# Order of the query tiles in a causal attention stage: each head from its longest row block to its shortest

## The reference

```python
q = (x @ Wq.T).reshape(B, T, H, hd)
...
q = _rmsnorm(q, gq)
k = _rmsnorm(k, gk)
...
scores = jnp.einsum('bhqd,bhkd->bhqk', q, k) * scale
...
scores = jnp.where(mask[None, None], -jnp.inf, scores)
attn = jax.nn.softmax(scores.astype(jnp.float32), axis=-1).astype(q.dtype)
out = jnp.einsum('bhqk,bhkd->bhqd', attn, v)
out = out.transpose(0, 2, 1, 3).reshape(B, T, H * hd)
return out @ Wo.T
```

## Time and profile before

| what | value |
|---|---|
| median of 3 runs | 1378.33 us (1376.38 to 1378.66) |
| the profiled execution, its own time | 1382.27 us |
| its span, first to last instruction | 1380.5 us |
| mean granted TensorE clock | 0.942 of full speed |
| PE busy | 1231.5 us, 89% of the span |
| PEld busy | 946.4 us, 69% |
| DVE busy | 962.3 us, 70% |
| ACT busy | 707.0 us, 51% |
| POOL busy | 552.5 us, 40% |
| chain that ended last | PE 54%, DVE 29%, issue 9%, ACT 5% |

### The profile page before, as it was taken

How to read it: one execution, slowest core, us unless ns; L and a number is a source line. 1 busy time by engine, 2 the same in 40 slices (tenths; PEclk the granted TensorE clock), 3 DMA queues, 4 the chain that set the end, 5 groups by cost and what they waited for, 6 DMA issues and landing times.

```text
span 1380.5 us, 24347 instructions
## 1 busy us (share of the span) xinstructions
PE 1231.5 (89%) x7708; PEld 946.4 (69%) x7708; DVE 962.3 (70%) x2821; ACT 707.0 (51%) x1639; POOL 552.5 (40%) x509
## 2 busy tenths in 40 slices
PE   6889888886469999999989999999998999999998
PEld 5435454443447787777877877778786788777787
DVE  5766777765467868778778678686677676675553
ACT  3354645455336456465464565554564654645442
POOL 0200000000038988898889888887802200000000
PEclk9799898888579999999999999999999999999999
DMA  6411011001110002101102001012001100000000
GB/s 216 123 30 46 24 43 55 24 32 62 61 55 23 32 11 101 41 0 41 41 10 91 21 27 39 8 38 96 4 30 62 34 32 23 8 0 1 16 16 31
DMA packets 31893, 56.85 MB, mean 41 GB/s; under 512 B 7096, under 2 KB 23328, under 8 KB 31312
## 3 DMA queue, kind: packets, MB, share of 16 engines
q1 hardware_dynamic: 27696, 42.93, 9.3%
q0 software_dynamic: 2976, 8.90, 2.2%
q10 hardware_dynamic: 1152, 4.19, 0.8%
HBM read 44.23 MB, written 11.66 MB: 40 GB/s over the span
## 4 chain that ended last, share of the span: by engine, by line
PE 54%; DVE 29%; issue 9%; ACT 5%; DMA 1%; SPq 1%; DVEq 0%; ACTq 0%
PE bank L1364 11%; PE bank L1342 7%; PE bank L278 6%; PE bank L280 6%; PE bank L279 6%; DVE qkst L1022 5%; DVE qk L1041 4%; PE bank L1353 4%; PE bank L1332 2%; DVE negmax L968 2%; PE bank L1277 2%; PE bank L1246 2%; DVE negmax L1054 2%; ACT hN L326 2%; PE bank L1264 1%
## 5 line engine op out<-in xcount | busy, mean ns | idle before, releaser
L574 POOL TENSOR_SCALAR gtmp<-gidx,lut 128x344 f32<-128x344 int32 (+2 forms) x210 | 302.8, 1442 | 21.3
L577 POOL TENSOR_TENSOR gacc<-gacc,gtmp 128x344 f32<-128x344 f32 (+2 forms) x210 | 183.4, 874 | 17.5
L1342 PE MATMUL bank<-kT,qT 128*128 128x128 f32 (+3 forms) x512 | 179.8, 442 | 9.4 <-ACT probs L776 9.4
L1364 PE MATMUL bank<-pT,v 128*128 128x128 f32 x1280 | 155.5, 277 | 12.3 <-ACT pT L769 12.3
L776 ACT ACTIVATE probs<-bank,negmax 128x128 f32<-128x128 f32 (+3 forms) x256 | 135.6, 530 | 53.6 <-DVE negmax L1054 50.9
L1054 DVE TENSOR_REDUCE negmax<-bank 128x1 f32<-128x128 f32 (+3 forms) x256 | 123.6, 485 | 54.9 <-PE bank L1343 53.5
L1364 PEld LDWEIGHTS bank<-pT,v 128*128 128x128 f32 x1280 | 148.0, 192 | 16.2 <-DVE oL L1064 14.9
L968 DVE TENSOR_REDUCE negmax<-bank 128x1 f32<-128x512 f32 (+3 forms) x176 | 108.9, 636 | 67.5 <-PE bank L1266 66.6
L1022 DVE BATCH_NORM_STATS2 qkst<-qk 128x6 f32<-128x128 f32 x512 | 110.2, 281 | 61.7 <-issue 61.6
L278 PE MATMUL bank<-wgH,hL 128*128 128x512 f32 x384 | 152.9, 398 | 0.2 <-issue 0.2
L280 PE MATMUL bank<-wgH,hH 128*128 128x512 f32 x384 | 153.0, 399 | 0.0
(11 more groups left out here) (215 smaller groups left out, 2707.2 us busy)
## 6 DMA issues: line engine op xcount, KB each, us to landing
hH<-h_saved SPq DMA_DIRECT2D x16, 512.0 KB, 3.8
hL<-h_saved SPq DMA_DIRECT2D x16, 512.0 KB, 4.8
qst<-q_parts SPq DMA_DIRECT2D x96, 64.0 KB, 2.3
wg<-in_wqkv SPq DMA_DIRECT2D x4, 1536.0 KB, 8.3
gate<-gates POOLq DMA_DIRECT2D x4, 512.0 KB, 7.0
wo<-in_wo SPq DMA_DIRECT2D x4, 512.0 KB, 9.1
out<-x SPq DMA_DIRECT2D x8, 256.0 KB, 2.1
wmod<-in_wmod SPq DMA_DIRECT2D x1, 1536.0 KB, 10.7
```

Of the source, the lines that this page charges most:

```text
L574: link(pool.tensor_scalar(tmp if j else acc, part, float(j), lut1[0:rows, j:j + 1], ALU.is_equal, ALU.mult))
L577: link(pool.tensor_tensor(acc, acc, tmp, ALU.add))
L1342: pe.matmul(bank[SCORE_BANKS[i % 3]][:, 0:n], qT[:, h, t * P:n], kT[:, h, 0:n], start=True, stop=False)
L1364: last = pe.matmul(bank[7][:, t * P:(t + 1) * P], v1[:, k, h * HD1:(h + 1) * HD1], pT1[:, h % 2, at:at + P], start=(k == 0), stop=(k == t))
```

## The change

A function `item1` gives the head and the tile of an item; t now goes 3, 2, 1, 0 within a head. All three engines use it: for the number of columns, for the place in `pT1`, and for the number of transposes. Slots, lags, buffers and the tests `i % QT == QT - 1` for the last item of a head stay. The wait of the first scores on `tr_act` is now one wait, at item 0, for all 8 steps.

```diff
+def item1(i):
+
+    return i // QT, QT - 1 - i % QT
...
-                        h, t = i // QT, i % QT
+                        h, t = item1(i)
                         act.wait_ge(t1_pe, it * ITEMS + i + 1)
                         act.wait_ge(pv1, it * HG + max(h - 1, 0))
                         at = t * (t + 1) // 2 * P
...
-                        n = (i % QT + 1) * P
+                        n = (item1(i)[1] + 1) * P
                         act.wait_ge(max1, it * ITEMS + i + 1)
...
-                        n = (i % QT + 1) * P
+                        n = (item1(i)[1] + 1) * P
                         dve.wait_ge(rsum1, it * ITEMS + i + 1)
...
-                        i, n = s, (s % QT + 1) * P
+                        i, n = s, (item1(s)[1] + 1) * P
                         dve.wait_ge(s1_pe, it * ITEMS + i + 1)
...
-                        i, h, t = s, s // QT, s % QT
+                        i, (h, t) = s, item1(s)
                         n = (t + 1) * P
-                        if i < QT:
-                            pe.wait_ge(tr_act, it * 2 * QT + 2 * (t + 1))
+                        if i == 0:
+                            pe.wait_ge(tr_act, (it + 1) * 2 * QT)
                         pe.wait_ge(exp1, it * ITEMS + max(i - 2, 0))
...
-                        t = i % QT
+                        t = item1(i)[1]
                         if i == 0:
                             pe.wait_ge(x1_add, it * 2)
```

## The result

The changed kernel takes **1457.01 us** (median of 6 runs, 1449.63 to 1457.99) against 1377.36 us for the kernel before (6 runs, 1375.29 to 1380.63). The ratio is 1.0558, with a 95% interval of 1.0540 to 1.0575. It is 79.6 us slower by the medians; the ratio and its interval make it 76.9 us (74.4 to 79.2), so the medians stand just above its upper edge. The forecast was 1438 us in a range of 1407 to 1460: the sign, the mechanism and the range held, and the forecast of +59.5 us was 20 us short of the difference of the medians.

The account below looks back on a forecast made before the run. TensorE bounds the kernel, never waiting within a head. Terms +32.5, +19.7, +18.9, -17.0 and +5.4 us sum to +59.5 us, taking the median of 1378.33 to 1437.8, taken as 1438 us; range 1407 to 1460.

Parts of the forecast that it names:

- the quiet terms: Costs without GpSimd over 16 rounds: starts +32.5 us, third heads +19.7 us, fourth heads with the end +18.9 us.
- the terms for GpSimd: Old starts' idle time where VectorE is late given back, -17.0 us; 512-column scalings slowed beside GpSimd, +5.4 us.
- the rival with GpSimd in the way: Every 512-column scaling in 11 rounds takes 1.08 instead of 0.49 us, 26 instead of 5.4 us: 1458 us; chance 8%.
- Cover of T3: 512-column item's transposes, within a head: due 3.06 us after its scores start instead of 5.29, as PV now follows them.
- Chain with `oH` and `oL` ahead of the scaling: 512-column softmax from the third head on: transposes start 4.29 us after the scores instead of 3.06; TensorE waits 1.23 us.
- The rival "`oH` and `oL` not on the path": Both slip beside the softmax chain, so the 512-column transposes wait 0.32 us in every head: 1409 us; chance 8%.
- End of a round, +1.18 us: Last head's 512-column scores to the last PV's end: 11.49 instead of 10.31 us, as the last PV waits for oL.
- Start, +2.03 us: Round's start: 512-column scores come first and need all copies; third head begins 2.03 us later, +32.5 us in 16 rounds.
- "Less what the old starts lose": Round starts where VectorE is late: 9.4 us before scores and most of 10.3 us behind the scaling go, -17.0 us.
- GpSimd's +5.4 us: 512-column scaling beside GpSimd takes 610 instead of 487 ns, on the path four times in each of about 11 rounds.
- The last round: a term put at nothing: Next stage's norm in the same queues, before and after: costed at nothing, bound of a microsecond or two.
- No loss of clock: TensorE waits of 1.2 us in 32 heads and 1.4 us at round ends are too short to lower the clock.

Follow-up runs that it names:

- run 8: Both kernels with 15 of the 16 GpSimd table entries left out of the feed-forward weights: kernel before 1351.58 us, changed kernel 1430.00 us.
- run 1: Changed kernel with oL one slot later on VectorE, behind the 512-column scaling instead of ahead of it: 1455.83 us.
- runs 3 and 4: Changed kernel with PV in two banks by turns and, in the first, oL one slot later (1430.36 us); in the second, oH and oL two slots later (1419.00 us).
- runs 6 and 7: Changed kernel with, in the first, only each round's first head in the old order (1427.89 us); in the second, only that head in the new order (1398.30 us).

## Why the prediction was right, and 20 us short

The mechanism was right, to some hundredths of a microsecond in a quiet head; the size of the sum was not. Its 59.5 us become the measured 79.6 by four parts: +7.4 in the quiet terms, +6.8 in the terms for GpSimd, +1.2 ahead of the rounds, and +4.7 because the profiled execution of before stood above its median. The measured 1457 is also what the rival with GpSimd in the way had (1458). That is a coincidence of numbers: by that rival GpSimd would add 26 - 17 = 9 us net to the difference, and run 8 puts it between -5 and +1.

- **Cover of T3, 3.06 us after S3 instead of 5.29: right.** T3 waits 1.05 us by the profile's count, 1.2 against the pitch of a queue without gaps, and a head takes 7.00 to 7.01 where 6.97 was forecast.
- **Chain with `oH` and `oL` ahead of the scaling: right as a reading of the path**, T3 at 4.28 against 4.29. What the prediction didn't see is that the single PV bank is a second limit of the same height: run 1 took `oL` out of the chain, the head stayed at 7.07 to 7.16 us and nothing was gained; runs 3 and 4 took both and gained 27 and 38 us. The rival "`oH` and `oL` not on the path" was priced at 1409; the nearest run, with both out of it, gave 1419.
- **End of a round, +1.18 us with the fourth head's wait inside it: right.** Third to last PV is 4.52 us, and the steps gave 9.26 - 4.74 = 4.52.
- **Start, +2.03 us: a little small.** In quiet rounds the last copy of k to the first PV takes 7.95 us; the steps gave 7.71. I had taken the pitch of a queue without gaps. The first S3 takes 1.02 us to the next start (1244.11 to 1245.13, below) instead of 0.91, and a T3 behind a wait up to 0.04 us more than its 0.45. In all, the quiet terms were 71.1 us, and the traces without lookups show 78.5: a quiet round costs 4.8 instead of 4.4 us, which is 5 of the 7 us, and the last round 6.3.

```profile
1244.11 1.13 PE L1347 MATMUL bank<-kT,qT 128*128 128x512 f32 x2 [0.83 <-ACT kT L765]
...
1245.13 0.86 PE L1347 MATMUL bank<-kT,qT 128*128 128x384 f32 x2
...
1246.88 0.49 PE L1347 MATMUL bank<-kT,qT 128*128 128x128 f32 x2 [0.29 <-ACT probs L781]
...
1247.65 0.63 PE L1358 MATMUL bank<-identf,probs 128*128 128x128 f32 x4 [0.22 <-issue]
```

- **"Less what the old starts lose", -17.0 us: the step that failed.** The size of the old loss was right: 110.1 - 92.2 = 17.9 us in the starts. Wrong was "there the new S3 comes no later than the first maximum allows", as if the new start had no such loss. It has 135.9 - 129.4 = 6.5 us of its own, so 11.4 came back and not 17.0. Ahead of the starts (first column) the new order loses another 1.4 us more than the old.
- **GpSimd's +5.4 us: the size held.** Between the PV the new order loses 2.9 and 3.6 us to GpSimd, the old one 0.7, 0.1 and 0.5, net 5.2; the forecast had the first two heads in it as well, whose part lies in the 6.5 us above. But the way was not an even one. In some rounds the scaling that T3 waits for falls beside GpSimd's work head after head, and lasts 1.12 us each time:

```profile
552.67 1.12 DVE L1054 TENSOR_SCALAR probs<-probs,rsum 128x512 f32<-128x512 f32 x1
...
560.33 1.12 DVE L1054 TENSOR_SCALAR probs<-probs,rsum 128x512 f32<-128x512 f32 x1
```

  These two are one head apart, and T3 waits 1.70 us in both. Both later heads were hit in rounds 3, 4 and 6 of the sixteen and one of them in some others, not all four scalings in all eleven rounds as the rival for GpSimd assumed. The net of the two GpSimd terms was forecast at -11.6 us; it is -4.8 by the rounds of the four traces and +1.2 by the medians of the four kernels.
- **The last round: a term put at nothing.** The prediction gave the norm of the next stage a bound of a microsecond or two. That round costs 6.3 instead of a quiet round's 4.8 us. Four of the norm's instructions stand ahead of `oH` on ScalarE, and T3 waits 3.01 us:

```profile
1314.70 2.06 ACT L331 ACTIVATE hN<-x,sm 128x256 f32<-128x256 f32 x4
1318.42 1.11 PE L1358 MATMUL bank<-identf,probs 128*128 128x128 f32 x4 [3.01 <-DVE probs L1054]
```

- **No loss of clock: right for the waits that were priced, not for the last round.** Waits of 1.05 to 1.70 us now come in the third and fourth heads. The granted clock reads 1.00 between 500 and 600 us, where a round with two waits of 1.70 us lies, and 0.99 between 700 and 1000 us, that is, the upper level of 2.4 GHz:

```profile
500.00:600.00 100.00, 88.92 (x545) 72.17 (x544) 71.28 (x210) 46.58 (x113) 88.53 (x74) 1.00 0.14 49
700.00:1000.00 300.00, 268.37 (x1636) 215.50 (x1636) 213.80 (x648) 149.40 (x376) 254.16 (x246) 0.99 0.09 31
```

  By the section "A second HAM failure mode: psum-queue depth-cycling" of the Trainium skill's "TensorE: Matmul & The Clock Gate" such gaps would make the clock swing. This trace does not agree. The clock did fall at the start of all four groups, as before, behind idle times of 2.5 to 2.7 us at 414, 654 and 1122 us and of 1.82 us at 889. It fell once more within the last round, behind the 3.01 us, which the prediction had named as a sign of being wrong:

```profile
416.00:421.00 5.00, 5.00 (x27) 4.72 (x25) 4.28 (x6) 3.48 (x6) 4.73 (x4) 0.57 0.03 12
892.00:894.00 2.00, 2.00 (x11) 1.83 (x11) 2.00 (x4) 1.27 (x3) 1.90 (x2) 0.50 0.02 6
1318.00:1320.00 2.00, 1.58 (x8) 1.58 (x9) 1.82 (x7) 1.24 (x5) 0.00 (x0) 0.51 0.00 0
```

  From 1320 to 1322 us it reads 0.64 and then 1.00 again, so this cost at most 2 x 0.49 + 2 x 0.36 = 1.7 us. The prediction's argument that 1.82 us passed "without a loss" was a misreading: the four transposes right behind it ran fast, but in the trace of before too the clock then stood at 0.50:

```profile
854.00:856.00 2.00, 2.00 (x11) 2.00 (x10) 2.00 (x3) 1.39 (x3) 1.81 (x3) 0.50 0.32 131
```

  That waits of 1.2 us would cost nothing was therefore less well founded than it reads, and in part luck.

What stays open is why runs 6 and 7 do not add up beside GpSimd; running those two without the lookups was not tried.

## What to carry to other kernels

In a hand-written software pipeline the order of items changes no work, only which long matmul block stands between an item's first and its last touch. Before reordering, write down for the longest item when its last step is due and how long its chain takes, with every foreign instruction that stands in the chain's queues; 0.3 us of missing cover and two helpers of 0.6 us in the wrong slots made half of the 80 us here, and the longest item at the start of each round the other half. When an edit that ought to take a wait away changes nothing, look at the trace before giving up the theory: the wait may have moved by one instruction to a buffer that was a hair behind it.

## What was not expected of the hardware

The slowing of VectorE's scaling beside GpSimd is not spread evenly. In the old order 512-column scalings had a mean of 610 ns between 640 and 760 us; in the new order it is 803 ns in the same window:

```profile
L1054 DVE TENSOR_SCALAR probs<-probs,rsum 128x512 f32<-128x512 f32 x8 | 6.4, 803 | 0.1
```

What counts is which of GpSimd's two instructions stands beside it. The two scalings of 1.12 us above (at 552.67 and 560.33) each start 0.07 us behind one of its additions:

```profile
552.60 0.91 POOL L582 TENSOR_TENSOR gacc<-gacc,gtmp 128x344 f32<-128x344 f32 x1
560.26 0.91 POOL L582 TENSOR_TENSOR gacc<-gacc,gtmp 128x344 f32<-128x344 f32 x1
```

In the whole changed trace 16 scalings of 512 columns start while such an addition runs; they take 0.55 to 1.12 us and end 0.28 to 0.29 us after it. Twenty lie beside GpSimd's other instruction alone (L579, one tensor and a scalar); 18 of these take 0.48 to 0.49 us, as with GpSimd silent. VectorE's maximum of 512 columns, which reads PSUM, takes 0.69 us with and without such an addition beside it. Three of GpSimd's pairs of instructions last 7.66 us (552.60 to 560.26), and so does a head whose scaling is slowed, instead of 7.01. So the next scaling starts 0.07 us behind an addition again, and the same instruction is hit head after head.

The Trainium skill's "GPSIMD Engine Reference", section "1. Specifications", says that GpSimd shares its SBUF interfaces with VectorE, with contention where VectorE's instruction is in a 2-port mode or has two SBUF inputs. The trace agrees that the two engines get in each other's way; in which mode the scaling runs no run here shows. Without the lookups every quiet head was 7.01 us.
